# Linear attention and mixture of experts on one core: attention in chunks of 64 tokens, with the keys of both heads of a pair on 128 partitions

## The chip, the cores and the metric

The kernel runs on one core of a Trainium2 chip. The metric is the device time of one execution in microseconds (us). The kernel before takes 1035.94 us (median of three runs, 1035.77 to 1036.93).

## The reference, cut to what matters

The input is 16 batches of 512 tokens with 256 channels, f32. Each batch goes through a causal linear attention of 16 heads of 16 channels and then through a router with 8 experts and a shared one.

```
x = x + attn(layernorm(x));  x = x + ffn(layernorm(x))
attn: q, k = elu(x Wq^T) + 1, elu(x Wk^T) + 1;  v = x Wv^T
      kv_sum += k_i v_i^T;  k_sum += k_i               # over the tokens i, in order
      out_i = (q_i kv_sum) / (q_i . k_sum + 1e-8);  then out Wo^T
ffn:  scores = sigmoid(x gate_w^T); 2 of 4 groups, then 4 of 8 experts by scores + bias
      sum over experts of weight_e * (silu(x Wg_e) * (x Wu_e)) Wd_e  + the shared expert
```

## The kernel before, in words

**Precision.** Projections and experts split each f32 operand into a high and a low part and make three products (`product`, L989). The attention's own products (`scores`, `values`, `state`, `inter`) and the router are plain f32 matmuls; the profile records each of these twice.

**Attention by chunks.** A batch is cut into 4 chunks (`SUBS`) of 128 tokens. Keys `kf` and queries `qf` lie as channel x token in two halves m of 128 channels; four pairs g of heads make a half, 32 partitions each. For a batch:

- `scores` i (0 to 3: half m, two chunks), L1098: for each chunk and g, the 32 rows of `kf` against two copies of the queries, each with one head of the pair zeroed (`q_half`, made on ACT by `q_split`, L636). Output 128 keys x 2 heads x 128 queries; the four g use four row tiles of TensorE and four banks of PSUM.
- `mask` (16 a batch): one 128x512 product with the causal mask from PSUM to one of `SM` = 8 slots of `scores` (DVE L860, in the opening list partly ACT and POOL).
- `state` i (a half each), L1085: `k_tok` (keys as token x channel) times `v_win`, for chunks 0 to 2. DVE then applies the block mask and sums over the chunks (L839, L845, L848) into `st`.
- `values` i, L1114: for each chunk, head and g, 128x32 weights from `v_win` (values with a window of zeros) against the masked scores; four column tiles.
- `inter` i, L1128: `st` against the queries, one 128x128 matmul a chunk, added in the same bank as values (`o`, one bank a half).
- The divisor goes `cum` (scan over k), `qk` (POOL), `den`, `wide`, `spread`; `mult` applies it, `at` splits the result, `wo` projects.

Keys as token x channel come from `blocks.2` (DVE), `put.2` and `get.2` (through `k_dram`), or in the opening list from `k_turn` (TensorE transposes, L1075).

**Order.** Five in-order lists of entries `name.i.lag` say what each engine does: an opening list (FIRST: batches 0 to 2), a list repeated 13 times (STEP; lag is how many batches behind), and a closing list (LAST). `warm.n` is n transposes of a constant (L1034) that compute nothing used. Six banks of PSUM are shared by all entries by the table `BANK`; an entry waits for the previous user of its bank to be drained. `load_x`, `put`, `get`, `cw_store`, `cw_load` and `store` are DMAs issued from SP's list in order.

Of the kernel before, what the change touches and what calls it, by code (L numbers as in the profile page):

```python
# [7 lines left out]
H, DH = 16, 16  # L8
# [14 lines left out]


ET, HR, CW, SM, XB = 3, 3, 4, 8, 2
# [27 lines left out]
        wo.0.2 wo.1.2 ln2_stats.0.2 mask.7.1 mask.5.1 ln2_apply.0.2 blocks.1.2 mask.6.1 mask.4.1 ln1_stats.0.0
        gate.6.3 gate.8.3 up.8.3 up.6.3 gate.7.3 state.1.1 blocks.0.0 up.7.3 mask.11.1 mask.8.1 mask.10.1
        mask.9.1 mask.12.1 mask.15.1 mask.14.1 mask.13.1 router.0.2 spread.0.1 route.0.2 gate.0.2 spread.1.1
        gate.1.2 mult.1.1 mult.0.1 rank0.0.2 rank1.0.2 k.0.0 up.0.2 gate.2.2 cum.0.0 q.0.0 up.2.2 k.1.0 up.1.2
# [10 lines left out]
        turn.0.0 turn.1.0 warm.17.0 v.1.0 k.0.0 q.0.0 v.0.0 k.1.0 q.1.0 scores.0.0 k_turn.0.0 scores.1.0  # L67
        warm.8.0 turn.0.1 turn.1.1 k_turn.1.0 state.0.0 values.0.0 scores.2.0 inter.0.0 values.1.0 scores.3.0
        k.0.1 q.0.1 inter.1.0 state.1.0 values.2.0 values.3.0 q.1.1 inter.2.0 scores.0.1 inter.3.0 warm.10.0
        k.1.1 wo.0.0 wo.1.0 scores.1.1 k_turn.1.1 v.1.1 v.0.1 k_turn.0.1 values.0.1 state.0.1 scores.2.1  # L70
        state.1.1 turn.3.0 inter.0.1 turn.2.0 inter.1.1 values.1.1 scores.3.1 gate.1.0 router.0.0 gate.0.0
# [6 lines left out]
        q_split.0.0 q.1.0 mask.1.0 v.0.0 mask.3.0 k_turn.0.0 ln1_apply.0.1 mask.7.0 piece.6.0 turn.0.1
        turn.1.1 mask.5.0 q_split.1.0 k_turn.1.0 wide.0.0 mask.9.0 mask.11.0 mask.13.0 piece.7.0 mask.15.0
        k.0.1 q.0.1 wide.1.0 at.0.0 q_split.0.1 q.1.1 mask.1.1 mask.3.1 at.1.0 k.1.1 mask.5.1 mask.7.1  # L80
        q_split.1.1 k_turn.1.1 v.1.1 v.0.1 k_turn.0.1 mask.9.1 mask.11.1 piece.8.0 turn.3.0 turn.2.0 mask.13.1
        ln1_apply.0.2 gate.1.0 wide.0.1 mask.15.1 gate.2.0 turn.0.2 gate.0.0 piece.9.0 wide.1.1 route.0.0
# [1118 lines left out]
```

## Time and profile before

| | us |
|---|---|
| median of the runs | 1035.94 |
| the profiled execution | 1035.56 |
| its span | 1033.8 |
| PE, DVE, POOL, ACT busy | 1007.7, 873.0, 537.8, 422.6 |

The span runs from the first to the last instruction; the profiled execution's time holds 1.8 us more. Engines are PE (TensorE's matmuls), PEld (its weight loads), DVE (VectorE), ACT (ScalarE), POOL (GpSimd) and SP (the DMA queue's engine). Matmuls overlap, so the pace of a group is read from the starts of two groups, not from a record's duration.

### The profile page before, as it was taken

Reading aid. Unit: us, or ns where it says so; the run is one execution under the profiler, and the core shown is the slowest. Engines: PE = TensorE matmul, PEld = TensorE weight load, DVE = VectorE, ACT = ScalarE, POOL = GpSimd, SP = SyncE. Lnnn points to the kernel's source line nnn. Section 1 sums busy time; section 2 is a strip of 40 time slices with the busy share of each in tenths; the row PEclk is TensorE's granted clock in tenths of the full one; section 3 lists DMA queues with packets and bytes.
Section 4 is the critical chain, followed back from the end, with each engine's and each line's share of the span. In section 5 each row is a group of like instructions: output and inputs, shape, how many; then the busy total and the mean of one; then the engine's idle time right before and its main releaser. Section 6 shows DMA issues by size and latency. Waiting matters only on the chain.

```text
span 1033.8 us, 22214 instructions
## 1 busy us (share of the span) xinstructions
PE 1007.7 (97%) x8437; PEld 858.1 (83%) x8437; DVE 873.0 (84%) x1855; ACT 422.6 (41%) x750; POOL 537.8 (52%) x440
## 2 busy tenths in 40 slices
PE   6889999999999999999999999999999999999997
PEld 5667878888888888888888888888888888888886
DVE  5988998898888889989898988889889898887564
ACT  5755343443434344343444434244343434422222
POOL 5763545636455564445646454564445546443653
PEclk9999999999999999999999999999999999999999
DMA  5011424444242443324435252443424345241511
GB/s 204 2 47 43 106 60 133 83 103 111 60 138 63 132 105 96 100 63 134 83 103 113 58 138 63 142 94 99 100 64 136 76 103 113 58 118 36 130 60 64
DMA packets 235161, 96.49 MB, mean 93 GB/s; under 512 B 161712, under 2 KB 217520, under 8 KB 235056
## 3 DMA queue, kind: packets, MB, share of 16 engines
q1 hardware_dynamic: 235056, 95.07, 36.0%
q8 instruction: 68, 1.11, 0.5%
q14 instruction: 37, 0.30, 0.1%
HBM read 66.60 MB, written 28.44 MB: 92 GB/s over the span
## 4 chain that ended last, share of the span: by engine, by line
PE 87%; DVE 6%; DMA 2%; ACT 1%; issue 1%; POOL 1%; SPq 1%; DVEq 0%; ACTq 0%
PE bank L989 53%; PE y_bank L989 19%; PE bank L1098 6%; PE bank L1114 5%; PE bank L1085 2%; PE bank L1128 2%; PE bank L1140 1%; DMA cw_all<-cw_dram 1%; DMA cw_all<-in_w_qkvo 1%; DVE scores L860 1%; DMA x_dram<-blocks 0%; DMA expo<-x_dram 0%; DVE den L869 0%; POOL et L729 0%; DVE et L957 0%
## 5 line engine op out<-in xcount | busy, mean ns | idle before, releaser
L989 PE MATMUL bank<-xt_hi,wg_hi 128*128 128x512 f32 x576 | 237.1, 412 | 3.0 <-DVE et L957 2.3
L989 PE MATMUL bank<-xt_hi,wg_lo 128*128 128x512 f32 x576 | 228.1, 396 | 0.0
L989 PE MATMUL bank<-xt_lo,wg_hi 128*128 128x512 f32 x576 | 227.8, 396 | 0.0
L732 POOL TENSOR_TENSOR h_lo<-et,h_hi 128x512 fp32r<-128x512 f32 x142 | 181.1, 1293 | 89.6 <-ACT h_hi L682 89.4
L729 POOL TENSOR_TENSOR et<-et,cw_all 128x512 f32<-128x512 f32 x126 | 166.2, 1338 | 112.6 <-DVE et L963 94.4
L860 DVE TENSOR_TENSOR scores<-bank,cst 128x512 f32<-128x512 f32 x240 | 152.6, 681 | 35.6 <-PE bank L1098 29.4
L989 PE MATMUL y_bank<-wd_hi,h_hi 128*128 128x256 f32 x576 | 164.9, 286 | 0.0
L989 PE MATMUL y_bank<-wd_lo,h_hi 128*128 128x256 f32 x576 | 162.1, 281 | 0.0
L989 PE MATMUL y_bank<-wd_hi,h_lo 128*128 128x256 f32 x576 | 161.3, 280 | 0.0
L989 PEld LDWEIGHTS bank<-xt_hi,wg_hi 128*128 128x128 f32 x576 | 108.3, 188 | 41.3 <-issue 16.6
L682 ACT ACTIVATE h_hi<-et 128x512 fp32r<-128x512 f32 x144 | 86.1, 624 | 116.7 <-POOL et L729 55.9
L957 DVE SCALAR_TENSOR_TENSOR et<-et,bank 128x512 f32<-128x512 f32 x144 | 95.9, 677 | 40.8 <-ACT et L673 40.7
L989 PEld LDWEIGHTS bank<-xt_hi,wg_lo 128*128 128x128 f32 x576 | 108.4, 188 | 26.0
L717 POOL TENSOR_TENSOR cum<-cum,qf 128x512 f32<-128x512 f32 x32 | 41.2, 1286 | 161.7 <-DVE qf L816 157.2
L989 PEld LDWEIGHTS bank<-xt_lo,wg_hi 128*128 128x128 f32 x576 | 108.8, 189 | 19.7
L673 ACT ACTIVATE et<-bank 128x512 f32<-128x512 f32 x144 | 82.1, 592 | 91.2 <-PE bank L989 58.4
L989 PEld LDWEIGHTS y_bank<-wd_hi,h_hi 128*128 128x128 f32 x576 | 108.5, 188 | 7.5 <-issue 4.0
L989 PEld LDWEIGHTS y_bank<-wd_lo,h_hi 128*128 128x128 f32 x576 | 108.4, 188 | 2.8
L989 PEld LDWEIGHTS y_bank<-wd_hi,h_lo 128*128 128x128 f32 x576 | 108.6, 189 | 0.0
L963 DVE SCALAR_TENSOR_TENSOR et<-et,bank 128x512 f32<-128x512 f32 x144 | 95.0, 678 | 13.5 <-PE bank L989 9.7
L636 ACT ACTIVATE q_half<-qf,cst 128x512 f32<-128x512 f32 x64 | 42.6, 714 | 118.3 <-PE bank L1098 117.6
L1098 PE MATMUL bank<-q_half,kf 32*128 32x256 f32 x1024 | 73.3, 400 | 2.8 <-DVE st L839 1.1
(135 smaller groups left out, 1870.5 us busy)
## 6 DMA issues: line engine op xcount, KB each, us to landing
cw_all<-cw_dram SPq DMA_DIRECT2D x128, 256.0 KB, 3.9
x_dram<-blocks SPq DMA_DIRECT2D x112, 128.0 KB, 3.3
out_y<-x_mid SPq DMA_DIRECT2D x32, 256.0 KB, 4.8
x_in<-in_x SPq DMA_DIRECT2D x15, 512.0 KB, 5.3
num_t<-x_dram SPq DMA_DIRECT2D x15, 512.0 KB, 4.0
expo<-x_dram SPq DMA_DIRECT2D x13, 512.0 KB, 4.0
k_dram<-blocks SPq DMA_DIRECT2D x52, 96.0 KB, 2.6
k_tok<-k_dram SPq DMA_DIRECT2D x13, 384.0 KB, 3.4
```

The costliest lines, as they stand in the source:

```text
L636: nc.scalar.activation(q_half[:, j, :], qf[:, i, :], ACT.Copy, scale=cst[:, C_EO + j:C_EO + j + 1]).then_inc(q_half_done, 1)
L673: nc.scalar.activation(et[:, i % ET, :], bank[BANK["gate", i]][:, :], ACT.Tanh, scale=0.5)\
L682: nc.scalar.activation(h_hi[:, i % HR, :], et[:, i % ET, :], ACT.Copy).then_inc(h_hi_done, 1)
L717: nc.gpsimd.tensor_tensor(cum[:, i, :], cum[:, i, :], qf[:, i, :], ALU.mult).then_inc(qk_done, 1)
L729: nc.gpsimd.tensor_tensor(et[:, i % ET, :], et[:, i % ET, :], weights, ALU.mult).then_inc(weighed, 1)
L732: nc.gpsimd.tensor_tensor(h_lo[:, i % HR, :], et[:, i % ET, :], h_hi[:, i % HR, :].bitcast(f32), ALU.subtract).then_inc(h_lo_done, 1)
L860: nc.vector.tensor_tensor(scores[:, i % SM, :, :], bank[BANK["scores", i]][:, :].rearrange("p (h q) -> p h q", h=4), causal.unsqueeze(1).b ...
L957: nc.vector.scalar_tensor_tensor(et[:, i % ET, :], et[:, i % ET, :], 1.0, bank[BANK["gate", i]][:, :], ALU.add, ALU.mult)\
L963: nc.vector.scalar_tensor_tensor(et[:, i % ET, :], et[:, i % ET, :], 0.5, bank[BANK["up", i]][:, :], ALU.mult, ALU.mult)\
L989: ins = nc.tensor.matmul(dst, l, r, start=first and n == 0, stop=last and n == 2, skip_group_check=shared)
L1098: last = nc.tensor.matmul(bank[BANK["scores", 4 * i + g]][:, j * 2 * P:(j + 1) * 2 * P] .rearrange("p (h q) -> p h q", h=2), kf[rows, m, c ...
L1114: last = nc.tensor.matmul(bank[BANK["o", m]][32 * g:32 * g + 32, c * P:(c + 1) * P], v_win[:, c, 4 * m + g, h:h + 2, :].rearrange("p t d - ...
```

## The change

The chunk becomes 64 tokens (`CH`), 8 chunks (`CHUNKS`) a batch, and the two heads of a pair lie together.

- `scores` i is a half of the batch, all 8 chunks: weights are `k_half`, 64 keys of one head and 64 of the other (128 columns), made on ACT by `k_split` in place of `q_split`; queries are used as they are. Eight masks a batch instead of 16, six slots instead of eight, used in turn over the batches (`ring`).
- `values` i is a half, one matmul a chunk and g: `v_pair` holds a pair's values in two blocks of 64 partitions. ACT fills it with four copies of 64 partitions for each v (two entries a batch); so for `k_turn`.
- `state` is one entry, one bank: 7 chunks x 2 halves x 4 pairs, 32x32 outputs. Its DVE work becomes a copy, sums over the chunks and one product with `head_mask`.
- `inter` i is 7 chunks x 4 pairs, 32x32 weights on the tiles (g, g).
- `get.2` is four DMAs, `put.2` moves 128 KB a piece instead of 96. The last batch's `cw_load` 4 to 7 go to the slots of scores.
- All lists and the bank table are new. The opening list of PE has 215 warm transposes instead of 35.

```diff
-ET, HR, CW, SM, XB = 3, 3, 4, 8, 2
+CH = P // 2
+CHUNKS = S // CH
+ET, HR, CW, SM, XB = 3, 3, 4, 6, 2
 STEP = { "PE":
-        up.5.3 wo.1.2 wo.0.2 down.0.3 down.1.3 scores.1.1 gate.6.3 down.2.3 gate.8.3 up.8.3 gate.7.3 up.7.3
-        up.6.3 down.3.3 state.1.1 down.4.3 scores.2.1 values.0.1 values.1.1 down.5.3 inter.0.1 inter.1.1
-        scores.3.1 gate.0.2 router.0.2 values.2.1 values.3.1 gate.1.2 up.0.2 inter.2.1 inter.3.1 gate.2.2
-        k.0.0 q.0.0 k.1.0 up.2.2 down.6.3 up.1.2 q.1.0 down.7.3 down.8.3 scores.0.0 up.4.2 v.1.0 v.0.0
-        gate.4.2 gate.5.2 state.0.0 gate.3.2 up.3.2
+        wo.1.2 up.5.3 wo.0.2 down.0.3 down.1.3 gate.8.3 down.2.3 gate.6.3 up.6.3 gate.7.3 down.3.3 state.0.1
+        values.0.1 down.4.3 up.8.3 up.7.3 scores.1.1 down.5.3 down.6.3 router.0.2 values.1.1 inter.0.1
+        inter.1.1 gate.2.2 gate.1.2 up.1.2 up.0.2 up.2.2 gate.0.2 k.0.0 q.0.0 down.7.3 k.1.0 scores.0.0
+        down.8.3 q.1.0 v.1.0 v.0.0 gate.3.2 up.4.2 gate.4.2 up.3.2 gate.5.2
 FIRST = { "PE":
+        turn.1.0 turn.0.0 warm.17.0 v.1.0 k.0.0 q.1.0 q.0.0 k.1.0 v.0.0 k_turn.0.0 warm.40.0 scores.0.0
+        warm.10.0 turn.0.1 turn.1.1 warm.11.0 k_turn.1.0 warm.22.0 scores.1.0 values.0.0 state.0.0 k.0.1 v.0.1
+        q.0.1 values.1.0 inter.0.0 inter.1.0 k.1.1 warm.21.0 wo.1.0 k_turn.0.1 wo.0.0 v.1.1 q.1.1 warm.9.0
+        k_turn.1.1 warm.14.0 turn.3.0 state.0.1 turn.2.0 warm.27.0 router.0.0 gate.1.0 scores.0.1 turn.0.2
+        gate.2.0 warm.13.0 turn.1.2 up.1.0 up.2.0 k.0.2 scores.1.1 values.0.1 up.0.0 k.1.2 inter.0.1
+        values.1.1 v.1.2 gate.0.0 q.0.2 inter.1.1 warm.17.0 scores.0.2 q.1.2 k_turn.1.2 k_turn.0.2 warm.14.0
+        up.4.0 v.0.2 gate.3.0 up.3.0 gate.4.0 gate.5.0
...
 # ACT: v, k_split
+                    for r in range(2):
+                        for h in range(2):
+                            last = nc.scalar.activation(
+                                v_pair[CH * h:CH * h + CH, 4 * i + r:4 * i + r + 3:2, :, DH * h:DH * h + DH],
+                                vals[CH * r:CH * r + CH, :, :, h, :], ACT.Copy)
...
+                    for j in range(2):
+                        nc.scalar.activation(k_half[:, :, j, :], kf[:, i, :].rearrange("p (c n) -> p c n", n=CH), ACT.Copy,
+                                             scale=cst[:, C_EO + j:C_EO + j + 1]).then_inc(k_half_done, 1)
...
 # DVE: state
+                    nc.vector.tensor_copy(st_sum[:, 0, :], sums[:, 0, :])
+                    link(nc.vector.tensor_copy(st_sum[:, 1:6:2, :], sums[:, 1:6:2, :]))
+                    link(nc.vector.tensor_tensor(st_sum[:, 1:6:2, :], st_sum[:, 1:6:2, :], sums[:, 0:5:2, :], ALU.add))
+                    link(nc.vector.tensor_tensor(st_sum[:, 3, :], st_sum[:, 1, :], st_sum[:, 3, :], ALU.add))
+                    link(nc.vector.tensor_tensor(st_sum[:, 5, :], st_sum[:, 3, :], st_sum[:, 5, :], ALU.add))
+                    nc.vector.tensor_tensor(st_sum[:, 2:7:2, :], st_sum[:, 1:6:2, :], sums[:, 2:7:2, :], ALU.add)\
+                        .then_inc(drained[BANK["state", 0]], 1)
+                    nc.vector.tensor_tensor(st[:, :, :, :].rearrange("p c m n -> p (c m) n"), ... head_mask ..., ALU.mult)
...
 # PE: state, scores, values, inter
+                    for c, m, g in product_range(CHUNKS - 1, KC, 4):
+                        last = nc.tensor.matmul(bk[32 * g:32 * g + 32, CH * c + 32 * m:CH * c + 32 * m + 32],
+                                                k_tok[:, m, c, 32 * g:32 * g + 32], v_pair[:, c, 4 * m + g, :],
+                                                start=True, stop=True)
...
+                    for c, g in product_range(CHUNKS, 4):
+                        rows, cs = slice(32 * g, 32 * g + 32), slice(CH * c, CH * c + CH)
+                        last = nc.tensor.matmul(bank[BANK["scores", 4 * i + g]][:, cs], k_half[rows, c, :, :].rearrange("p t n -> p (t n)"), qf[rows, i, cs],
+                                                start=True, stop=True)
...
+                    for c, g in product_range(CHUNKS, 4):
+                        last = nc.tensor.matmul(bank[BANK["o", i]][32 * g:32 * g + 32, CH * c:CH * c + CH],
+                                                v_pair[:, c, 4 * i + g, :], ring(4 * i + g, b)[:, c, :],
+                                                start=(c == 0), stop=False, skip_group_check=True)
...
+                    for c, g in product_range(CHUNKS, 4):
+                        if c > 0:
+                            rows, cs = slice(32 * g, 32 * g + 32), slice(CH * c, CH * c + CH)
+                            last = nc.tensor.matmul(bank[BANK["o", i]][rows, cs], st[rows, c - 1, i, :], qf[rows, i, cs],
+                                                    start=False, stop=True, skip_group_check=True)
```

## Rows read from the trace of the kernel before

**Rows 1.** The page: busy time of PE; the chain that ended last, by engine.
```profile
PE 1007.7 (97%) x8437; PEld 858.1 (83%) x8437; DVE 873.0 (84%) x1855; ACT 422.6 (41%) x750; POOL 537.8 (52%) x440
...
PE 87%; DVE 6%; DMA 2%; ACT 1%; issue 1%; POOL 1%; SPq 1%; DVEq 0%; ACTq 0%
```

**Rows 2.** Windows: busy us (records), sum of five steps from 438.79 to 747.86.
```profile
sum 309.07, PE 308.81 PEld 263.98 DVE 271.79 ACT 126.84 POOL 158.75; mean PE 61.76 PEld 52.80 DVE 54.36 ACT 25.37 POOL 31.75
```

**Rows 3.** Waits of PE from 130 to 880: us in total, times, longest.
```profile
PE bank L989 <- DVE qf L816: 1.0, 1, 1.0
...
```

**Rows 4.** Windows (PE, PEld, DVE, ACT, POOL, granted clock, DMA) and timeline, opening.
```profile
0.00:105.00 105.00, 87.25 (x823) 71.42 (x824) 85.42 (x173) 61.62 (x107) 64.12 (x54) 1.00 0.22 74
...
6.95 3.67 PE L1003 MATMUL bank<-cst 128*128 128x128 f32 x16 [6.95 <-DMA wr<-in_w_router]
...
11.70 2.02 PE L1034 MATMUL y_bank<-cst 128*128 128x128 f32 x17
...
104.25 0.49 PE L1075 MATMUL bank<-cst,kf 128*128 128x128 f32 x3
```

**Rows 5.** Timeline of PE: start, us until the group's modelled end.
```profile
503.85 0.83 PE L1128 MATMUL bank<-qf,st 128*128 128x128 f32 x6
504.61 1.15 PE L1098 MATMUL bank<-q_half,kf 32*128 32x256 f32 x16
505.69 0.50 PE L989 MATMUL bank<-xt_hi,wg_hi 128*128 128x512 f32 x1
...
506.96 0.40 PE L989 MATMUL bank<-xt_hi,wg_lo 128*128 128x512 f32 x1
...
507.75 1.93 PE L1114 MATMUL bank<-scores,v_win 128*32 128x128 f32 x64
509.61 0.50 PE L989 MATMUL bank<-xt_hi,wg_hi 128*128 128x512 f32 x1
...
536.31 0.91 PE L1085 MATMUL bank<-v_win,k_tok 128*128 128x128 f32 x6
536.97 0.48 PE L989 MATMUL bank<-xt_hi,wg_hi 128*128 128x512 f32 x1
```

**Rows 6.** Timeline of PE, 507.74 to 507.77 only.
```profile
507.75 0.29 PE L1114 MATMUL bank<-scores,v_win 128*32 128x128 f32 x4
```

**Rows 7.** Groups by shape, 200 to 800: busy us, mean ns, idle before.
```profile
L1114 PEld LDWEIGHTS bank<-scores,v_win 128*32 128x32 f32 x1164 | 31.4, 110 | 3.0 <-issue 3.0
...
L1085 PEld LDWEIGHTS bank<-v_win,k_tok 128*128 128x128 f32 x114 | 14.6, 191 | 2.6 <-issue 2.2
```

**Rows 8.** Waits in PE's queue, windows 507.52 to 507.60 and 507.97 to 508.0.
```profile
L1110 PEldq EVENT_SEMAPHORE  x1: 51/51/51, 507.5 to 507.5; - x1
...
L1107 PEldq EVENT_SEMAPHORE  x1: 51/51/51, 508.0 to 508.0; - x1
```

**Rows 9.** Groups by shape, 200 to 800, of DVE and ACT.
```profile
L860 DVE TENSOR_TENSOR scores<-bank,cst 128x512 f32<-128x512 f32 x152 | 96.6, 681 | 23.2 <-PE bank L1098 18.9 <-PE bank L1114 3.7
...
L616 ACT ACTIVATE v_win<-bank 128x512 f32<-128x512 f32 x20 | 12.0, 598 | 42.5 <-PE bank L989 42.5
...
L839 DVE TENSOR_TENSOR st<-bank,cst 128x384 f32<-128x384 f32 x19 | 10.5, 554 | 2.2 <-PE bank L1085 1.9
L833 DVE STREAM_TRANSPOSE blocks<-kf 128x384 f32<-128x384 f32 x20 | 10.1, 542 | 0.0
...
L845 DVE TENSOR_TENSOR st<-st 128x128 f32<-128x128 f32 x19 | 7.3, 384 | 0.7
...
L848 DVE TENSOR_TENSOR st<-st 128x128 f32<-128x128 f32 x19 | 5.5, 292 | 0.7
...
L666 ACT ACTIVATE sig<-logit 128x32 f32<-128x32 f32 x9 | 2.1, 230 | 18.1 <-DVE logit L924 18.1
```

**Rows 10.** The key transfer: SP's queue at 532.9, and the page's DMA issues.
```profile
532.89 0.38 SPq L548 DMA_DIRECT2D k_tok<-k_dram  x1
...
k_tok<-k_dram SPq DMA_DIRECT2D x13, 384.0 KB, 3.4
```

More of the change, by code:

```diff
@@ L51 @@
+        weigh.2.2 split.0.2 split.1.2 qk.1.0
         """,
     "DVE": """
[L53 to L56, printed above, removed]
@@ L66 @@
     "PE": """
[L67 to L71, printed above, removed]
@@ L78 @@
[L78 to L82, printed above, removed]
@@ L83 @@
-        at.0.1 turn.1.2 k.0.2 q.0.2 split.0.0 q_split.0.2 k.1.2 at.1.1 v.1.2 k_turn.0.2 v.0.2 q.1.2 split.1.0
-        gate.3.0 gate.4.0 split.2.0 k_turn.1.2 wide.0.2 gate.5.0 q_split.1.2
+        piece.0.0 piece.1.0 turn.1.0 turn.0.0 piece.2.0 piece.3.0 piece.4.0 k.0.0 v.1.0 q.0.0 k.1.0
+        k_split.0.0 piece.5.0 v.0.0 q.1.0 k_turn.0.0 ln1_apply.0.1 turn.0.1 piece.6.0 mask.3.0 k_split.1.0
+        mask.1.0 turn.1.1 k_turn.1.0 piece.7.0 mask.5.0 wide.1.0 mask.7.0 wide.0.0 k.0.1 q.0.1 at.0.0 at.1.0
@@ L85 @@
+        k.1.1 k_turn.0.1 k_split.0.1 v.1.1 v.0.1 k_turn.1.1 turn.3.0 q.1.1 wide.0.1 piece.8.0 turn.2.0
+        ln1_apply.0.2 mask.3.1 mask.1.1 turn.0.2 route.0.0 gate.2.0 gate.1.0 k_split.1.1 turn.1.2 k.0.2
+        mask.7.1 mask.5.1 k.1.2 at.0.1 k_split.0.2 wide.1.1 v.1.2 gate.0.0 q.0.2 piece.9.0 split.0.0
+        k_split.1.2 at.1.1 q.1.2 k_turn.1.2 split.1.0 split.2.0 v.0.2 gate.3.0 k_turn.0.2 wide.0.2 gate.5.0
+        gate.4.0
         """,
     "POOL": """
-        rstd1.0.0 piece.1.0 piece.2.0 piece.3.0 piece.4.0 piece.5.0 rstd1.0.1 qk.0.0 mask.1.0 mask.3.0
@@ L101 @@
+        mask.2.2 mask.3.2 q.1.2 mask.1.2 den.0.2 cum.1.2 den.1.2 gate.3.0 gate.4.0 up.3.0 gate.5.0 up.5.0
         up.4.0
@@ L190, in fills, with product_range @@
     if name == "values":
-        return [("o", i // 2)] if i % 2 == 0 else []
+        return [("o", i)]
     return [(name, i)] if name in BANKED else []
+def product_range(*sizes):
+    return itertools.product(*(range(n) for n in sizes))
 def nth(engine, names, per=1):
@@ L388, in linear_attention_moe @@
         got = [sem("x1_got"), sem("x2_got"), sem("k_got")]
-        GOT = [nth_of("SP", "get", i, 16) for i in range(3)]
+        GOT = [nth_of("SP", "get", i, 64 if i == 2 else 16) for i in range(3)]
         taken_hi, TAKEN_HI = sem("taken_hi"), nth("ACT", ("take",))
@@ L830, in _ @@
                         src = kf
-                    n = (SUBS - 1) * P if i == 2 else S
                     for j in range(2):
-                        last = nc.vector.transpose(blocks[:, j * n:(j + 1) * n], src[:, j, 0:n])
+                        last = nc.vector.transpose(blocks[:, j * S:(j + 1) * S], src[:, j, :])
                     last.then_inc(blocked, 1)
                 elif name == "state":
-                    dve.wait_ge(filled, FILLED["state", i, b])
-                    wait_filled(dve, "inter", 2 * i, b - 1)
@@ L1078, in _ @@
                     if b in TURNED[2]:
-                        pe.wait_ge(drained[BANK["k_turn", i]], USES["k_turn", i, b])
+                        for j in range(KC):
+                            pe.wait_ge(drained[BANK["k_turn", j]], USES["k_turn", j, b])
                     else:
@@ L1122, in _ @@
[L1122 to L1130 removed]
+                    pe.wait_ge(drained[BANK["q", i]], USES["q", i, b])
```

343 lines of the change are left out of this document (162 added, 181 removed).

## The prediction

> **What bounds the kernel now.** I read the page first: TensorE (PE) is busy 97% of the span and carries 87% of the chain that ended last, where VectorE (DVE) has 6% [rows 1]. Then the stretches. From 438.8 to 747.9 us, five steps of the repeated list (one step is one batch), PE is busy 61.76 of 61.8 us a step, DVE 54.4 and ScalarE (ACT) 25.4 [rows 2]. So in the steady steps PE has no idle time at all and a step lasts as long as PE's own work; removing DVE work there is worth nothing by itself. The list of waits says the same: from 130 to 880 us PE waits in three places, at most 1.0 us [rows 3]. The first 105 us are different: PE is idle 105 − 87.3 = 17.8 us there, 7.0 of it before its first instruction [rows 4]. The opening list ends about 104.5 us, with its last k_turn [rows 4]. So I need (a) the PE cost of attention for a batch, before and after, and (b) what the opening list does.
>
> **PE, attention of one batch, before.** Each f32 matmul shows as two records.
> - scores: an inter entry of 6 records starts at 503.85, the 16 records of scores at 504.61, the next gate at 505.69 [rows 5]. The six take 0.66 (6 × 0.11, as the six of state, 536.31 to 536.97, do), so scores cost 1.84 − 0.66 = 1.18. Four entries: 4.7.
> - values: 64 records, two entries, from 507.75 to 509.61, so 1.86; four: 3.7.
> - state and inter: 12 records each, 0.11 apiece: 1.3 and 1.3.
> - Sum 11.1 us of the 61.8.
>
> **What sets a record's pace.** The 64 values records are 16 rounds over four column tiles of 32 [rows 5]. Seventeen warm transposes, also 128 f32 columns, took 2.02 with the last one's tail of 0.27, so 0.109 each [rows 4]; 16 rounds at that pace are 1.74, and the 0.12 left is the change of tile shape. A look of 0.03 us wide finds all four records of a round, which together last 0.29 us while one lasts 0.273: they start within 0.02 us and run side by side [rows 6]. A state record of 128 columns also paces at 0.11. So the pace is that of the moving columns (0.85 to 0.9 ns each in f32), and four tiles share it. A scores entry is four rounds of 256 columns on four row tiles: 4 × 0.215 = 0.86, and 0.32 for filling and for changing the tile shape. A weight load of 128 columns lasts 0.191, one of 32 columns 0.110 [rows 7]: 96 columns make 0.08, so loading 128 columns takes about 0.11 of stream and 32 about 0.03, the rest being latency. State's records load 128 columns and pace at 0.11, so the load runs under the previous matmul.
>
> **PE, after.**
> - scores: 2 entries of 32 matmuls, 16 rounds of 64 columns on four row tiles, each with a load of 128 columns. Moving takes 0.056, but the load needs 0.11: the load sets the pace. 16 × 0.11 + 0.32 = 2.08; twice 4.2. Half the columns, almost no gain.
> - values: 128 records of 64 columns with loads of 32: 32 rounds × 0.056 = 1.8.
> - inter: 7 chunks × 4 tiles × 2 halves × 2 = 112 records, 28 rounds × 0.056 = 1.6.
> - state: 112 records of 32 columns, 28 rounds. Floor 0.03 by columns. Ceiling by how fast PE's queue can be fed: between a wait of values' line L1110 at 507.52 and the next one of L1107 just before 508.0 lie 32 matmul and 32 load records, at most 0.48/64 = 0.0075 each [rows 8], so 0.060 for a round of eight. 0.8 to 1.7; I take 1.2, since the queue is full when state begins.
> - changes of tile shape, 0.12 each by values: about three more edges than before, 0.3.
> - Sum 9.1: **2.0 us less a batch**, bounds 1.5 and 2.6. Values, inter and state together go from 6.4 to 4.6 although their records go from 152 to 352.
>
> Here a rule speaks against the change. The rows show four records starting in 0.02 us on different tiles [rows 6], and none of under 128 columns. The Trainium skill ("TensorE: Matmul & The Clock Gate", section Back-to-back issue gap) says that starts never come closer than about 25 ns, however few the columns. By it values, inter and state would be 352 × 0.025 = 8.8, an estimate, and the change would lose 2.2 us a batch; the trace contradicts it for different tiles and is silent for the rest.
>
> **Other engines in a step.** DVE: eight masks fewer, 8 × 0.681 = −5.4; the old state (2 × (0.554 + 0.384 + 0.292) = 2.5) is replaced by one masked product of 448 columns (0.6), three operations of 192 (between the rows of 128 and 384 columns, about 0.4) and three of 64 (under 0.29, about 0.25): 2.5; blocks of the keys 2 × (0.68, as the mask, − 0.54) = +0.3 [rows 9]. Net −4.8, worth nothing under PE, but DVE goes to about 50 of 60. ACT: eight copies of 64 partitions × 256 for v instead of two of 0.598: between +0.6 (0.23 each, ACT's row of 32 elements) and +3.6 (0.598 each, as for 512); it has 36 us free a step, and if that cover were gone these 0.6 to 3.6 us would be paid. SP: three more issues for get.2, whose one issue takes 0.38 in SP's queue [rows 10], so about 1.2 us later for the cw_load behind it; these serve weigh one step later. The landing (896 KB for 384 KB, 3.4 us before) is hidden by the step between get.2 and state. POOL has no mask in the steps: nothing.
>
> New waits: scores.0 stands behind q.0, down.7 and k.1 after k.0. A product of this size takes 1.4 (a gate's first and sixth record start at 505.69 and 506.96 [rows 5], and each paces 0.24), so 4.2 of cover, against relu and exp on ACT, a DVE product and two k_split copies, with ACT's two of q.0 between: six of about 0.6, as v's, and one of 0.68, as the mask's [rows 9], 4.3. values.1 stands 3.3 us behind scores.1, against four masks of 0.68. Both are tight; I take +0.2 a step, bounds 0 and 1.4.
>
> **The opening list.** Projections, turns, gates and ups are the same in number. Warm transposes go from 35 to 215; at 0.109 each: +19.6. Six k_turns have a fourth transpose: +0.7. Attention up to there: 9 scores, 8 values, 5 state entries and two batches of inter, 24, become 5, 4, 2 and 2 batches, 20: −4. PE's work grows by 16.3. Waits: 10.7 us of idle time are there to be filled, and some 4 more lie under the modelled ends of records. If all vanish it is +2, if none +16; the warm entries stand where PE waits now (masks, wo, state), so I take **+6**.
>
> **Sum.** Opening +6; thirteen steps × (−2.0 + 0.2) = −23.4; the closing list −1.7. Span 1033.8 − 19.1 = 1014.7; with the 1.8 us between the profiled run's span and its time (1035.56, 0.4 under the median of the three runs) 1016.5, and I say **1016**. A change under 0.2% (2 us) can't be told from none here.
>
> **Rivals.**
> 1. *PE's small records have a floor.* If a record cannot pace below the 0.029 that values shows, values, inter and state cost 352 × 0.029 = 10.2, the batch 14.7: +3.6. 1033.8 + 6 + 47 + 3 + 1.8 = **1091**; it decides from 0.019 a record, where the batch breaks even. For it: no row has narrower records. Against: it is exactly the column pace, and the queue took 0.0075 each.
> 2. *Row tiles that write one bank take turns.* inter's four tiles read four row groups and write one bank, where scores' four write four banks. One after another, 112 × 0.055 = 6.2 for 1.6: +2.6 a batch, **1078**. The Trainium skill ("TensorEngine Tiling (Array Packing)", Restrictions and Gotchas) says different row tiles cannot access one bank at the same time. No row shows such a matmul. Against it stands that the outputs lie in different partitions, as values' do.
> 3. *scores' loads are not hidden.* Load and matmul in turn, 0.11 + 0.056 a round: +1.8 a batch, **1041**. Against: state's pace.
> 4. *The tight waits bind,* 1.4 a step: 1016 + 16 = **1032**.
>
> **How the numbers follow.** The forecast has 0.73 and its own range 1002 to 1030 (2.6 a batch and +2 in the opening; 1.5, 0.4 of waits and +12). Rival 1 has 0.10, rival 2 0.05, rival 3 0.05, rival 4 0.07. Reaching to rivals 3 and 4 the range is 1002 to 1044, which leaves out rivals 1 and 2 and little else. Faster 0.78 (forecast and most of rival 4), same 0.02, slower 0.20.
>
> **What would show it.** Steps of about 60.0 us with PE still without idle time; a values entry of 64 records in 0.9 and inter of 56 in 0.8; a scores entry in 2.1, with rounds of 0.11; state of 112 in 0.8 to 1.7; the opening list ending near 110 us. It is wrong if these entries last longer than the ones they replace, if PE waits in every step for kf, k_half or scores, or if the granted clock, now 1.00 throughout, falls in stretches of small tiles.

## The result: 0.85% slower

The changed kernel takes 1043.08 us (median of ten runs, 1039.55 to 1048.53), the kernel before 1034.73 in the runs beside it (1032.95 to 1036.93). The ratio is 1.0085, 95% interval 1.0063 to 1.0106. The forecast was 1016, range 1002 to 1044, with 0.78 on faster: the time is inside the range, the direction is wrong. The profiled execution took 1041.22, its span is 1039.4, 5.6 more than before. So the traces account for 5.6 of the 8.4 us between the medians. The other runs of the changed kernel were slower at a lower mean granted clock: 1039.55 and 1041.22 at 0.998, 1044.21 and 1047.22 at 0.992, 1048.53 at 0.989.

The page of the changed kernel, busy time and the DMA queues; it answers [rows 1].

```profile
PE 995.2 (96%) x12847; PEld 870.2 (84%) x12847; DVE 791.3 (76%) x1751; ACT 463.4 (45%) x856; POOL 533.5 (51%) x432
...
q1 hardware_dynamic: 262304, 103.51, 41.6%
q8 instruction: 101, 1.65, 0.7%
```

PE lost 12.5 us of work although its records rose from 8437 to 12847; DVE lost 82. Both went as meant, and the span still grew. One more row moved: q8, the queue that fetches instructions, has 101 packets where the kernel before has 68 (1.11 MB). One packet is 16,384 bytes; I read it as a block of 256 of PE's instructions (a matmul's record and its load's are two). The counts agree: PE has 26,035 records and semaphore instructions in the changed trace, 258 a packet, and 17,443 in the trace of before, 257 a packet.

The five steps that answer [rows 2]: windows from one first wo record to the next, with their sum.

```profile
427.79:489.50 61.71, 59.95 (x785) 52.30 (x784) 49.47 (x111) 27.41 (x51) 31.95 (x27) 1.00 0.48 111
489.50:550.80 61.30, 59.73 (x786) 52.26 (x785) 49.53 (x111) 27.41 (x51) 32.14 (x27) 1.00 0.47 110
550.80:611.30 60.50, 59.64 (x786) 52.15 (x785) 49.51 (x111) 27.40 (x51) 32.03 (x27) 1.00 0.49 113
...
sum 305.61, PE 298.69 PEld 261.10 DVE 247.50 ACT 137.05 POOL 160.14; mean PE 59.74 PEld 52.22 DVE 49.50 ACT 27.41 POOL 32.03
```

PE's work in a step is 59.74 us, 2.0 less than the 61.76 of before: that term is as forecast. But a step lasts 61.12 on average, because PE now stands still for 1.38 of it. Before, it stood still for 0.05. Over all 13 repetitions PE's work is 59.7 a step (61.8 before) and it stands still for 1.3 (0.2 before). The list of PE's waits from 130 to 900 us, which answers [rows 3], says at what:

```profile
PE bank L1148 <- issue: 8.8, 8, 1.6
PE bank L1159 <- issue: 5.4, 5, 1.6
PE y_bank L1027 <- issue: 1.8, 1, 1.8
```

"issue" is a stop with no semaphore behind it: 16.0 us in 14 stops, nearly all inside values (L1148) and inter (L1159), and no stop for kf, k_half or a mask. The timeline of PE shows one, and the queue view of 200.3 to 201.4 us shows what arrives then.

```profile
199.20 1.16 PE L1125 MATMUL bank<-v_pair,k_tok 128*32 128x32 f32 x112
200.49 0.76 PE L1148 MATMUL bank<-scores,v_pair 128*32 128x64 f32 x38
202.72 0.61 PE L1148 MATMUL bank<-scores,v_pair 128*32 128x64 f32 x26 [1.47 <-issue]
...
q8 instruction: 1, 0.02, 5.5%
```

After 38 of the 64 records of a values entry PE stops for 1.47 us, and an instruction packet that began at 200.34 ends in the trace 1.4 us before it goes on. Counting PE's records and waits from its first one, every such stop falls on the 193rd or 194th of a block of 256 (numbers 5313, 6849, 9154, 10690, 11713, ...): always on one border, a whole number of blocks apart. Counted the same way, these 12 largest stops (0.94 to 2.06 us from start to start) come where the 256 instructions up to the border were used up in 1.5 to 2.0 us. Three more borders with 2.0 us have 0.3 to 0.4 us, one with 2.1 has no stop, and neither has any other, all with 3.4 us or more. In the kernel before no 256 instructions take less than about 7.1 us, in the same part of the trace.

The packets' times show what PE waits for. Each of these 15 stops ends 1.3 to 1.6 us after the end of an instruction packet, and that packet began at most 1.2 us after PE had passed the border before. At the border with 2.1 us and no stop the packet had ended 4.9 us earlier. So the next block is fetched only about when the one before it is begun, and dense entries use a block up sooner than the next is ready.

The first wo record of a batch marks the lists: in the kernel before one stands 1.47 us after the start of the repeated list (its up.5 comes first), in the changed kernel it is the first record of the list. The two rows of before are the first of the first repetition and of the closing list, then the same two of the changed kernel, each from a timeline.

```profile
105.97 0.28 PE L989 MATMUL bank<-wa_hi,at_hi 128*128 128x256 f32 x1
...
912.30 0.28 PE L989 MATMUL bank<-wa_hi,at_hi 128*128 128x256 f32 x1
```

```profile
121.64 0.28 PE L1027 MATMUL bank<-wa_hi,at_hi 128*128 128x256 f32 x1
...
915.36 0.28 PE L1027 MATMUL bank<-wa_hi,at_hi 128*128 128x256 f32 x1
```

| us of the span | before | changed | difference | forecast |
|---|---|---|---|---|
| opening list | 104.5 | 121.6 | +17.1 | +6 |
| 13 repetitions | 806.3 | 793.7 | −12.6 | −23.4 |
| closing list | 123.0 | 124.0 | +1.1 | −1.7 |
| sum | 1033.8 | 1039.4 | +5.6 | −19.1 |

The opening and the stops in the steps are 11 us each off the forecast. The experiments are about these two.

### The profile page after: what moved, and what is told of

It is laid out like the page before. It is cut to its first block, busy times and chain, and to the rows that moved or that the text cites. A ratio compares the mean times of both kernels' runs of the same rounds, so it can differ in the third digit from the quotient of the medians.

```text
span 1039.4 us, 30806 instructions
## 1 busy us (share of the span) xinstructions
PE 995.2 (96%) x12847; PEld 870.2 (84%) x12847; DVE 791.3 (76%) x1751; ACT 463.4 (45%) x856; POOL 533.5 (51%) x432
## 4 chain that ended last, share of the span: by engine, by line
PE 90%; ACT 3%; issue 3%; DVE 2%; DMA 1%; SPq 0%; POOL 0%; DVEq 0%; ACTq 0%
PE bank L1027 54%; PE y_bank L1027 20%; PE bank L1135 6%; PE bank L1148 3%; PE bank L1159 3%; PE bank L1125 2%; PE bank L1170 1%; ACT v_pair L650 1%; ACT k_tok L678 1%; ACT k_half L669 1%; PE y_bank L1072 1%; DMA wr<-in_w_router 0%; DMA num_t<-x_dram 0%; PE bank L1041 0%; DMA x_dram<-blocks 0%
## 5 line engine op out<-in xcount | busy, mean ns | idle before, releaser
L1027 PE MATMUL bank<-xt_hi,wg_hi 128*128 128x512 f32 x576 | 230.4, 400 | 3.0 <-DVE et L995 1.2
L771 POOL TENSOR_TENSOR h_lo<-et,h_hi 128x512 fp32r<-128x512 f32 x142 | 187.2, 1329 | 83.6 <-ACT h_hi L721 83.6
L768 POOL TENSOR_TENSOR et<-et,cw_all 128x512 f32<-128x512 f32 x124 | 158.7, 1291 | 118.4 <-DVE et L1001 88.5
L756 POOL TENSOR_TENSOR cum<-cum,qf 128x512 f32<-128x512 f32 x32 | 46.0, 1437 | 131.2 <-DVE cum L893 131.2
L900 DVE TENSOR_TENSOR scores<-bank,cst 128x512 f32<-128x512 f32 x120 | 77.4, 684 | 39.0 <-PE bank L1135 35.1
L1135 PEld LDWEIGHTS bank<-qf,k_half 32*128 32x128 f32 x2048 | 60.3, 186 | 16.6 <-issue 16.2
L658 ACT ACTIVATE expo<-bank 128x512 f32<-128x512 f32 x64 | 38.3, 598 | 73.0 <-PE bank L1027 71.0
```

The costliest lines, as they stand in the source:

```text
L658: nc.scalar.activation(expo[:, e, :], bank[BANK[name, i]][:, :], ACT.Relu, scale=-1.0)\
L756: nc.gpsimd.tensor_tensor(cum[:, i, :], cum[:, i, :], qf[:, i, :], ALU.mult).then_inc(qk_done, 1)
L768: nc.gpsimd.tensor_tensor(et[:, i % ET, :], et[:, i % ET, :], weights, ALU.mult).then_inc(weighed, 1)
L771: nc.gpsimd.tensor_tensor(h_lo[:, i % HR, :], et[:, i % ET, :], h_hi[:, i % HR, :].bitcast(f32), ALU.subtract).then_inc(h_lo_done, 1)
L900: nc.vector.tensor_tensor(ring(i, b), bank[BANK["scores", i]][:, :].rearrange("p (a q) -> p a q", q=CH), causal.unsqueeze(1).broadcast_to( ...
L1027: ins = nc.tensor.matmul(dst, l, r, start=first and n == 0, stop=last and n == 2, skip_group_check=shared)
```

## The experiments

Each ratio is to the kernel before, run on the same chip. "Mark" is the first wo record of the second batch, 105.97 before and 121.64 in the changed kernel.

**few_warm.** The changed kernel with only one of its opening's twelve warm entries left (17 transposes of 215).

```diff
-        turn.1.0 turn.0.0 warm.17.0 v.1.0 k.0.0 q.1.0 q.0.0 k.1.0 v.0.0 k_turn.0.0 warm.40.0 scores.0.0
+        turn.1.0 turn.0.0 warm.17.0 v.1.0 k.0.0 q.1.0 q.0.0 k.1.0 v.0.0 k_turn.0.0 scores.0.0
...
```

> The changed kernel with the opening list's warm transposes cut from 215 to the first 17; nothing else. Theory A (the 198 transposes are work that PE would not have done, 198 x 0.109 = 21.6 us, and little of it lies under waits): the opening list ends 12 to 20 us earlier and the time falls to about 1026. Theory B (the opening list is held by ACT's copies, and the transposes stand mostly where PE would wait anyway): the opening list ends 0 to 6 us earlier, and PE's idle time there grows by 16 to 20 us. If the transposes hold the clock up, the granted clock in the opening falls below 1.00 and part of it is lost again.

1042.97 us, ratio 1.0074 (1.0056 to 1.0093): no gain from 198 transposes fewer. The mark is later, 127.3, where both theories had it earlier. Windows of 15 us of the opening (PE, PEld, DVE, ACT, POOL, granted clock, DMA), and PE's wait for `k_tok` up to 120 us:

```profile
15.00:30.00 15.00, 8.37 (x66) 7.15 (x65) 6.00 (x16) 13.54 (x27) 9.45 (x7) 0.90 0.23 84
30.00:45.00 15.00, 10.86 (x200) 9.85 (x200) 7.85 (x13) 8.50 (x16) 5.07 (x5) 0.50 0.01 1
45.00:60.00 15.00, 12.28 (x330) 10.42 (x322) 9.36 (x17) 6.07 (x10) 6.71 (x7) 0.92 0.01 3
60.00:75.00 15.00, 9.70 (x161) 7.86 (x159) 11.53 (x36) 13.01 (x26) 4.30 (x4) 0.76 0.16 46
...
PE bank L1135 <- ACT k_tok L678: 10.1, 2, 6.6
```

Without the transposes PE is busy 8.4 of 15 us, waits 10.1 us for k_tok (longest 6.6), and then the granted clock is 0.50, the lower of its two levels (1.2 GHz), for a whole window. Leaving the transposes out gives nothing back here, and this run doesn't price them.

**spread.** The changed kernel with the step's order changed so that entries with many small records stand apart.

```diff
 # PE, cut to the entries that moved
-  down.3.3 state.0.1 values.0.1 down.4.3 up.8.3 up.7.3 scores.1.1
-  values.1.1 inter.0.1 inter.1.1 gate.2.2 gate.1.2 up.1.2 up.0.2
+  down.3.3 state.0.1 down.4.3 up.8.3 values.0.1 up.7.3 scores.1.1
+  values.1.1 gate.2.2 gate.1.2 inter.0.1 up.1.2 inter.1.1 up.0.2
 # DVE
-  router.0.2 mult.1.1 mult.0.1 route.0.2 gate.1.2 gate.2.2 up.1.2 rank0.0.2
+  router.0.2 route.0.2 mult.0.1 gate.1.2 gate.2.2 up.1.2 mult.1.1 rank0.0.2
```

> The changed kernel with the repeated list of PE reordered so that the entries with many small records do not follow one another: two products between state and values.0, two between values.1 and inter.0, one between inter.0 and inter.1 (and DVE's two mult entries moved to match). Theory C (PE waits for its own instructions: all mid-entry gaps lie a multiple of 256 PE instructions apart, 128 matmul and load pairs, and two such borders never follow within 3 us without a gap): the gaps inside values and inter go from about 1.3 us a step to under 0.4, a step falls from 61.1 to about 60.2, and the time by 10 to 14 us. Theory D (the gaps come from something in the entries themselves: a bank, a semaphore, a reading engine): they stay at 1.3 us a step wherever the entries stand, and the time moves by less than 3 us.

1039.16 us, ratio 1.0027 (1.0016 to 1.0039). PE's waits from 130 to 900:

```profile
PE bank L1029 <- POOL xa_lo L747: 7.9, 13, 0.8
```

Every issue stop is gone, with the same instructions in another order, as theory C said. The time fell by less than its 10 to 14 us (1.0085 to 1.0027 of the kernel before). What is left is a new wait ahead of k.0 for POOL's half of `take`, in each of the 13 steps, which last 60.9.

**quarter_values.** The kernel before with each values matmul cut into four of 32 columns: the same arithmetic, four times the instructions of this entry.

```diff
-  bank[...][32 * g:32 * g + 32, c * P:(c + 1) * P], v_win[...], scores[..., :],
+  bank[...][32 * g:32 * g + 32, c * P + 32 * piece:c * P + 32 * piece + 32], v_win[...], scores[..., 32 * piece:32 * piece + 32],
```

> The kernel before with each values matmul cut in four of 32 columns: same data, banks, weights and sums, four times the records (512 instead of 128 a batch). By the pace of the changed kernel's state entry (a round of four tiles of 32 columns in 0.035 us) the columns cost 64 x 0.035 = 2.2 us for 1.86 a pair of entries, +0.7 a batch, +11 us in all. Theory C (a block of 256 PE instructions can't be had faster than about 3.3 us): a pair of entries is 1024 instructions fewer 512, that is 512 loads and matmuls, two blocks, so it can't take less than 3.3 to 5 us, with gaps of 1 to 2 us inside it: +2 to +5 us a batch, +30 to +80 us. Theory D: +11 us and no gaps inside.

1161.81 us, ratio 1.1223 (1.1199 to 1.1246), 125 us more, above even theory C's 30 to 80; steps of 67 to 73 us. Waits from 130 to 900, and a piece of the timeline:

```profile
PE bank L1114 <- issue: 51.4, 26, 2.8
```

```profile
215.81 1.22 PE L1114 MATMUL bank<-scores,v_win 128*32 128x32 f32 x117
...
217.89 1.47 PE L1114 MATMUL bank<-scores,v_win 128*32 128x32 f32 x127 [0.86 <-issue]
...
221.55 0.26 PE L1114 MATMUL bank<-scores,v_win 128*32 128x32 f32 x5 [2.19 <-issue]
```

In a kernel with nothing of the change in it the stops appear as soon as an entry is made of many small instructions. From the restart at 217.89 the next 256 instructions are used up in 1.3 us, and PE stops for 2.2. All 28 large stops between 130 and 900 us come after 256 instructions in 1.2 to 2.2 us, and where they took 3.2 or more there is none. Each ends 1.2 to 1.6 us after the end of an instruction packet, as in the changed kernel.

What the stops don't explain can be read from the same trace. In the 13 repetitions (113.60 to 1029.42 us, 109.5 longer than before) PE stops for 66.0 us at "issue", as its waits say; the last line is the window of this stretch:

```profile
PE bank L1114 <- issue: 60.6, 30, 2.8
PE y_bank L989 <- issue: 4.0, 2, 2.1
PE bank L989 <- issue: 1.4, 1, 1.4
...
113.60:1029.42 915.82, 849.60 (x11753) 730.89 (x11752) 742.47 (x1526) 326.11 (x585) 411.52 (x338) 0.96 0.35 88
```

Between the stops 256 values records take 2.55 us where 64 took 1.87, so the entries themselves cost 1.4 a batch, 18 in all. The third part is the clock: it was 1.00 before, and here the lower level was granted for 65 of the 916 us, which costs at most 32 by an estimate (half of 65). No run takes the clock's part by itself.

**few_warm_spread.** Both edits. 

> Both edits on the changed kernel. If the two losses are independent the savings add: with theories B and C about 1043 - 3 - 12 = 1028; with A and C about 1014; with B and D about 1040.

1044.38 us, ratio 1.0081 (1.0061 to 1.0101): none of the three sums came. The steps are 60.9 as in spread, the mark is 125.0. Beside spread, leaving the transposes out costs 0.5%.

**spread_take.** spread, and ACT's `take.1.0` ahead of `at.1.1`, so that k.0 is not kept waiting.

```diff
 # ACT
-  take.0.0 at.1.1 take.1.0
+  take.0.0 take.1.0 at.1.1
```

> The kernel of run spread with one more edit: ACT's repeated list takes take.1.0 before at.1.1. Run spread had no gaps inside its entries, but PE waited for xa_lo before k.0 in every step (7.9 us in 13 times, and longer counted from record to record, 1.0 us), which at.1.1 holds up ahead of take.1.0. Theory C (the changed kernel's PE work is a step of 59.9 us, and only instruction loading and this wait stand over it): a step falls from 60.9 to 59.7 to 60.1, the time by 11 to 15 us against spread, to about 1026, and it is faster than the kernel before. Rival E (another chain, of ACT, POOL or the transfers, has a period of about 60.9 by itself, since every step of spread is 60.9 to a tenth): the wait moves elsewhere and the time falls by less than 3 us.

1033.56 us, ratio 0.9976 (0.9967 to 0.9984): the first version faster than the kernel before, though the 5 us won on spread (1.0027 to 0.9976) are less than half of the 11 to 15 expected. Windows from 150 to 900 us:

```profile
sum 750.00, PE 748.12 PEld 642.93 DVE 626.15 ACT 341.08 POOL 393.71; mean PE 249.37 PEld 214.31 DVE 208.72 ACT 113.69 POOL 131.24
```

PE stands still for 1.9 of 750 us (15.5 in the changed kernel), and the step lasts 60.4. By its busy share that is 60.3 us of work where the changed kernel's order has 59.7: keeping small entries apart costs 0.6, which I put down to changes of tile shape (spread_join takes two of them back), and saves 1.3 of stops.

**kt_dve** and **spread_take_kt.** The changed kernel, and spread_take, with two of the four copies of each k_turn on DVE, for theories on the opening.

```diff
 # ACT: k_turn, two copies with no shift of partitions; DVE: a new entry k_turn
+                    nc.vector.tensor_copy(k_tok[0:CH, i, 1:CHUNKS - 1:2, :], rows_of[CH:P, 0:SUBS - 1, :])
+                    nc.vector.tensor_copy(k_tok[CH:P, i, 1:CHUNKS - 1:2, :], rows_of[CH:P, 0:SUBS - 1, :])
```

> The changed kernel with two of the four copies of each k_turn in the opening list made by DVE instead of ACT. Theory B (ACT holds the opening list: six k_turns of four copies, 2.2 us each against one of about 0.5 before): the opening list ends 3 to 8 us earlier. Rival F (the opening is held by PE's own work with the added transposes, or by DVE): it moves by less than 2 us, or comes later by up to 3.

> Spread_take and kt_dve together: if the opening and the steps are separate, the savings add, about 1026 - 5 = 1021 with theories C and B, 1026 with C and F.

1060.28 us (ratio 1.023) and 1049.33 (1.0127), both slower than every theory allowed; kt_dve's mark is 130.0, 8.4 later. PE's waits up to 140 us in kt_dve:

```profile
PE bank L1133 <- issue: 5.4, 2, 4.8
PE bank L1143 <- DVE k_tok L896: 3.9, 2, 2.7
PE bank L1035 <- DVE et L1003: 3.9, 1, 3.9
```

The copies are waited for as long as before (3.9), now at DVE, whose other work comes later too. The 4.8 us stop ahead of state stands at no border of 256; what it waits for isn't shown. Half the copies moved this way buy nothing; it doesn't show that the copies cost nothing.

**scores_first.** The changed kernel with scores.0.0 ahead of k_turn.0.0 and its 40 transposes.

```diff
-  v.0.0 k_turn.0.0 warm.40.0 scores.0.0 warm.10.0
+  v.0.0 scores.0.0 k_turn.0.0 warm.40.0 warm.10.0
```

> The changed kernel with scores.0.0 ahead of k_turn.0.0 (and its 40 transposes) in PE's opening list. Scores.0.0 then needs only k_half and q, ready about 24 us, and not the bank that ACT's four k_tok copies free at 29.5. If the first scores entry is on the chain that sets the opening's end, the opening ends 3 to 5 us earlier; if the opening is held by PE's added transposes or by work further on, it moves by less than 1 us.

1046.62 us, ratio 1.0098. The mark is 127.8, where 3 to 5 us earlier or no change was expected. The granted clock is 0.87, 0.79 and 0.77 between 15 and 60 us. The waits of the scores entries aren't shorter: 5.1 us for ACT's `v_pair` and `k_tok` where the changed kernel has 3.9 for `k_tok`. Whether the edit brought the lower clock isn't shown, since kernels with the changed opening got 0.75 in some executions too (spread_take, below under spread_join).

**before_warm, before_copies, before_warm_copies.** The opening can be taken apart from the other side, by putting its two additions into the kernel before: 178 more transposes; ACT's copies of v and k_turn cut into four of 64 partitions; both.

```diff
 # before_warm, PE's opening list, nine places such as
-        q.1.0 scores.0.0 k_turn.0.0
+        q.1.0 scores.0.0 warm.40.0 k_turn.0.0
 # before_copies, ACT: v (k_turn likewise, 4 x 64 x 192)
+                    for r in range(2):
+                        for s in range(2):
+                            last = nc.scalar.activation(v_win[64 * r:64 * r + 64, 2 * i + s, :, 0:3:2, :],
+                                                        vals[64 * r:64 * r + 64, s], ACT.Copy)
```

> The kernel before with warm transposes added to its opening list alone, 213 instead of 35, put beside the same kinds of entries as in the changed kernel; nothing else differs. They are 178 x 0.109 = 19.4 us of TensorE work. Theory W (waits aren't filled): TensorE's waits in the opening are links of a chain that runs through ACT and DVE, so what is put ahead of one of its entries only pushes the chain on; the opening list ends 14 to 19 us later, the steps keep 62.0 us, the time is 1050 to 1055. Rival (waits are filled, as the prediction reckoned with): most of the 10.7 us of waits turns into transposes and the list ends 6 to 9 us later, 1042 to 1045.

> The kernel before with ACT's copies cut as in the changed kernel: each copy of v into four of 64 partitions x 256, each copy of a k_turn into four of 64 partitions x 192; the same data goes to the same place. By the changed kernel's rows a v takes 4 x 0.38 = 1.5 us for 0.6, a k_turn about 4 x 0.4 = 1.6 for 0.5, twelve of them in the opening: ACT +12. Theory C (ACT's copies hold up the opening): v_win and k_tok come 1 us later each time and TensorE waits for a good part of them, opening +4 to +8 us, steps unchanged, the time 1040 to 1044. Rival (ACT has room there): opening +0 to +2, within 0.2% of the kernel before. In the steps both expect nothing, since ACT has over 30 us a step free.

> Both edits together, in the kernel before. If transposes and copies each lie on the path, their costs add: theory W + C gives the opening +18 to +27, 1054 to 1062. If the added transposes give ACT time to copy (rival: one covers the other) the sum is the larger of the two alone, so about that of the transposes alone.

| | us | ratio (interval) | mark | later by |
|---|---|---|---|---|
| transposes | 1047.46 | 1.0113 (1.0095 to 1.0131) | 118.5 | 12.5 |
| copies | 1047.38 | 1.0110 (1.0092 to 1.0129) | 114.4 | 8.4 |
| both | 1052.64 | 1.0166 (1.0147 to 1.0185) | 121.4 | 15.4 |

Groups of ACT by shape, in before_copies up to 110 us; and one window of before_copies and of before_warm_copies each:

```profile
L619 ACT ACTIVATE v_win<-bank 64x256 f32<-64x256 f32 x24 | 7.7, 371 | 2.6 <-PE bank L993 2.4
...
L646 ACT ACTIVATE k_tok<-bank 64x192 f32<-64x192 f32 x20 | 6.5, 323 | 0.2
```

```profile
30.00:45.00 15.00, 12.35 (x148) 9.78 (x148) 11.14 (x20) 12.69 (x27) 8.23 (x7) 0.89 0.01 2
```

```profile
30.00:45.00 15.00, 13.40 (x177) 11.50 (x178) 7.91 (x15) 10.06 (x22) 5.88 (x6) 1.00 0.01 2
```

Three readings. The transposes alone cost 12.5 of their 19.4 us: a third fell into waits, two thirds pushed the chain on. The time moved by 12.4, between the rival's 6 to 9 and theory W's 14 to 19. A copy of 64x256, a quarter of the elements, takes 371 ns where one of 128x512 takes 598 [rows 9]; so a v costs 0.9 us more, a k_turn 0.8, together some 10 us of ACT in the opening, and 8.4 arrive at the mark, part of it perhaps the granted clock of 0.89 from 15 to 45 us. The time moved by 12, more than the 4 to 8 expected: in its profile the steps and the closing list are 3.2 longer as well, which isn't explained. These k_turn copies are also lighter than the changed kernel's, 1.3 us each where those take 2.2, so the run prices the copies too low. Together they cost 15.4 and not 20.9: where ACT copies longer, the transposes fill the wait and the clock stays at 1.00.

**spread_join.** spread_take with the two inter entries side by side again.

```diff
-  values.1.1 gate.2.2 gate.1.2 inter.0.1 up.1.2 inter.1.1 up.0.2
+  values.1.1 gate.2.2 gate.1.2 inter.0.1 inter.1.1 up.1.2 up.0.2
```

> spread_take with the two inter entries side by side again (inter.0.1 inter.1.1 up.1.2 in place of inter.0.1 up.1.2 inter.1.1), still apart from values. Two changes of tile shape fewer, 0.12 each: the step goes from 60.4 to 60.1 to 60.2 us, -3 us in all, 1030 to 1031 if no block of 256 instructions is used up in under 3.3 us. inter.0 and inter.1 are 224 instructions in 1.55 us and stand between entries of 12 to 24: 256 of them take about 3.0 us, so the rival is that issue gaps come back in some of the steps, up to 0.5 us each, and nothing is won: 1033 to 1036.

1034.48 us, ratio 0.9987 (0.9975 to 0.9999), not told apart from spread_take's. PE's waits from 130 to 900, and the windows from 150:

```profile
PE bank L1029 <- DVE kf L855: 6.1, 13, 0.7
```

```profile
sum 750.00, PE 743.90 PEld 643.87 DVE 626.34 ACT 344.12 POOL 394.13; mean PE 247.97 PEld 214.62 DVE 208.78 ACT 114.71 POOL 131.38
```

No issue stop came back in the steps, though 256 instructions are used up in 2.8 us at three borders; the 3.3 us that the expectation feared was too high. PE's work fell by 0.4 a step for the two shape changes, and a new wait of 0.5 for `kf` took it: a step is 60.4 again. This kernel's opening list is the changed kernel's, word for word, and its profiled execution had the full clock all through it: mark 118.9, against 121.6 in the changed kernel's (granted clock 0.89 from 45 to 60 us) and 124.0 in spread_take's (0.75 and 0.79 from 30 to 60). One opening list spans 5 us, and the granted clock is the difference that the traces show.

## Why the prediction was wrong, point by point

**PE's work of a batch: right.** The starts of consecutive groups in the changed kernel's timeline answer [rows 5]:

```profile
151.27 1.08 PE L1148 MATMUL bank<-scores,v_pair 128*32 128x64 f32 x64
152.28 2.14 PE L1159 MATMUL bank<-qf,st 32*32 32x64 f32 x112
154.35 0.50 PE L1027 MATMUL bank<-xt_hi,wg_hi 128*128 128x512 f32 x1
...
168.84 2.01 PE L1135 MATMUL bank<-qf,k_half 32*128 32x64 f32 x64
170.78 0.39 PE L1027 MATMUL y_bank<-wd_hi,h_hi 128*128 128x256 f32 x1
```

Values 1.01 an entry, scores 1.94, state 1.29 (199.20 to 200.49, above). Both inters take 2.07 here because a border costs 0.3 to 0.4 inside them (153.4 us); without one they take 1.70. With two scores and two values that is 8.9, shape changes included, for 9.1 forecast. Half the columns in scores won 0.8 us of 4.7 a batch (forecast 0.5): sixteen rounds at the load's 0.11 are 1.76 of an entry's 1.94, so the weight load paces it, as the prediction said.

**Rivals 1, 2 and 3: fell.** State's 112 records start within 0.967 us, 0.0087 each, a third of rival 1's 0.029 and below the 0.019 where it would decide. Inter, on four row tiles and one bank, takes 1.70 for 112 records where rival 2 had 6.2. The Trainium skill's two rules that were weighed ("TensorE: Matmul & The Clock Gate", section Back-to-back issue gap: at least about 25 ns between starts; "TensorEngine Tiling (Array Packing)", Restrictions and Gotchas: no common bank for row tiles at one time) don't describe matmuls on different tiles of this kernel. A scores entry is 1.94, with no load in turn (rival 3).

**The other engines: right, and worth nothing in the steps, as said.** DVE 49.50 for "about 50", ACT +2.0 within 0.6 to 3.6; a cover of over 30 us hides it. **Rival 4,** 1.4 a step for the tight waits for `kf`, `k_half` and masks, gave by chance the measured size with another cause: the list of waits has none of them. Its time (1032) missed, because the opening was also wrong.

**Step "thirteen steps × (−2.0 + 0.2)": failed in the 0.2.** It priced the semaphore waits of a step and left out PE's own supply of instructions. Measured over the 13 steps: −2.1 of work, +1.3 of stops at block borders (16.0 us in 770) in place of the 0.2 that PE had stood still before, so −1.0 a step and −12.6 in all. The stops end 1.3 to 1.6 us after an instruction packet has ended; spread, with the same instructions in another order and no stop, shows that their density is the cause, and quarter_values that the kernel before gets them too once its entries are dense. [rows 8] had misled me: as I now read it, 64 records in 0.48 us was what PE's queue could hand over from what it held, not what could be fetched. In all the runs there are stops where 256 instructions up to a border took 2.2 us or less and none where they took 2.5 or more; a few with 2.0 to 2.3 have none. My expectations had put it at 3.3, having counted the stop itself in. In spread_take no 256 take less than 2.8 us. The Trainium skill ("Runtime: NRT & Kernel Launch", section Instruction fetch mechanics) says the instructions come in 16 KiB blocks of 256 and that crossing a border is mostly hidden. The block size agrees with the packets of q8; "hidden" holds for the kernel before and not here, where the 12 large stops last 0.7 to 1.8 us and, in quarter_values, up to 2.8.

**Step "the opening list: +6, bounds +2 to +16": failed, +17.1.** Three terms of it:

- *The filled waits.* I let most of 16.3 us of added PE work vanish in 10.7 us of waits. PE's idle time up to 105 us was 17.8 [rows 4], and up to 120 in the changed kernel it is still 18.2:

```profile
sum 120.00, PE 101.78 PEld 90.08 DVE 74.33 ACT 74.96 POOL 55.97; mean PE 101.78 PEld 90.08 DVE 74.33 ACT 74.96 POOL 55.97
```

  So in sum none of the added work vanished in waits: 16.3 was forecast of it, and the list is 17.1 longer. before_warm has the size for the transposes: of 19.4 us of transposes 12.5 arrive. Work set ahead of a wait fills it only if what the wait is for doesn't itself start after that work.
- *ACT's copies.* v's were priced for the steps and called hidden; in the opening ACT is the second busiest link and they weren't priced at all, nor were k_turn's. One k_turn copy took 0.51 before; now four take 2.2, in ACT's timeline and in the list of PE's waits up to 120 us:

```profile
27.30 2.17 ACT L678 ACTIVATE k_tok<-bank 64x512 f32<-64x512 f32 x4
```

```profile
PE bank L1135 <- ACT k_tok L678: 3.9, 2, 2.3
```

  The second line is scores waiting, since `k_half` comes behind these copies on ACT or the bank is freed late: scores.0.0 starts at 29.68, at 24.65 before. On top of the transposes the copies cost 2.9, alone 8.4, in their lighter form.
- *The clock.* It was taken as 1.00. It is in the kernel before, but the new opening sometimes loses it: its mark is 2.8 us later in this profile than in spread_join's.

The pieces close roughly: 104.5 + 15.4 (transposes and copies) − 4 (attention) + 0.7 (k_turns) = 116.6; the full-clock opening ends at 118.9 and this one at 121.6. Two things can fill the 2.3 between 116.6 and 118.9. The k_turn copies are heavier than those that before_copies priced. And the stops at block borders are in the opening too, which neither the forecast nor the runs with the kernel before have: spread_join's PE stops for 2.0 us there and this one's for 2.3, the longer time inside state, on the 194th of a block again and 1.4 us after the end of a packet.

```profile
PE bank L1125 <- issue: 2.3, 2, 1.8
```

No run tells the two apart.

**Closing list: −1.7 forecast, +1.1 measured.** PE has five waits of 0.6 to 1.4 there, and had one of 2.3. But before_warm, whose closing list is that of before, is 2.3 us longer from its last mark to its last matmul, so a difference of this size isn't evidence. It stays open.

**What the change is worth.** With the step reordered it is 0.24% faster than the kernel before, not 1.9%: of the 2.0 us a step 0.6 go to shape changes, and the opening stays 14 to 19 longer (118.9 and 124.0 for 104.5). A lower-cost opening wasn't found; the five tries (fewer transposes, twice; copies on DVE, twice; scores first) were no better.

## What to carry to other kernels

- When an edit trades columns for instructions, count the instructions of each stretch and not only their pace: here 256 of PE's (a matmul's record and its load's are two) in 2.0 us or less nearly always meant a stop, of 0.3 to 3.1 us, and in 2.5 or more never. Put dense entries between sparse ones, and look whether a stop marked "issue" falls on one border of 256 and ends soon after an instruction packet.
- An opening is a chain through several engines. Price there each operation that the steady state hides, and ask of every wait to be filled whether what ends it starts behind the filler.
- Put the suspected addition into the old kernel. Taking it out of the new one (few_warm) changed the clock and told nothing; adding it to the old one gave a price.

## What the runs showed of the hardware

- 112 matmuls of 128x32 with 32 columns on four tiles start within 0.967 us, 0.0087 each; a round of four takes 0.035.
- Stops at borders of 256 instructions on PE: up to 1.8 us of idle time in the changed kernel and 2.8 in quarter_values, when 256 were used up in 2.2 us or less. PE went on 1.2 to 1.6 us after the end of the packet, at all 15 and 28 of them.
- In quarter_values, with 66 us of such stops in 916, the granted clock was at its lower level for 65 us; it was 1.00 over the same steps of the kernel before.
- ACT copies of 64 partitions: 323 ns for 192 columns, 371 for 256, 487 for 384 and 588 for 512, where one of 128x384 takes 496 and one of 128x512 takes 598. Halving the partitions saved next to nothing.
- The same opening list, with PE busy 12.7 of the 15 us before, got a clock of 1.00 from 30 to 45 us in one execution and 0.75 in another. The difference at the mark is 5 us (118.9 and 124.0), more than the change wins in its best order.
